# An attention and feed-forward block on one core: the steps written out over the images, another order around the taps, and one feature stream across images

## What is computed

```python
qkv = conv2d(layernorm_c(x), qkv_w)                    # 1x1, 768 channels
agg = conv2d(qkv, agg_dw_w, groups=768, padding=2)     # 5x5 depthwise
agg = conv2d(agg, agg_pw_w, groups=96)                 # 1x1, grouped
q, k, v = relu, relu, id of the thirds of concat(qkv, agg), heads of 8; v gets a column of ones
out = q @ (k^T v);  out = out[:-1] / (out[-1] + eps)
x = x + batchnorm(conv2d(out, proj_w))
t = layernorm_t(tokens of x)
w = expert weights from softmax(mean(t) @ router^T), top 2
x = x + sum_e w_e (gelu(t @ W1_e + b1_e) @ W2_e + b2_e)    # 6 experts, 341 wide
```

## Time and profile before

| | |
|---|---|
| device time, median of 3 runs | 1735.21 us |
| lowest, highest | 1733.52, 1737.08 us |
| span of the profiled execution | 1727.4 us (its own device time is not listed; the median is 7.8 us over the span) |
| mean granted clock of TensorE | 0.895 |
| PE busy | 1398.5 us, 81% |
| DVE busy | 1291.6 us, 75% |
| POOL busy | 1180.7 us, 68% |
| ACT busy | 931.2 us, 54% |
| chain that ended last | PE 44%, DVE 19%, POOL 18%, issue 13% |

### The profile page before, as it was taken

How to read it: one execution, slowest core, us unless ns; L and a number is a source line. 1 busy time by engine, 2 the same in 40 slices (tenths; PEclk the granted TensorE clock), 3 DMA queues, 4 the chain that set the end, 5 groups by cost and what they waited for, 6 DMA issues and landing times.

```text
span 1727.4 us, 20194 instructions
## 1 busy us (share of the span) xinstructions
PE 1398.5 (81%) x6652; PEld 793.5 (46%) x6652; DVE 1291.6 (75%) x1305; ACT 931.2 (54%) x1622; POOL 1180.7 (68%) x1017
## 2 busy tenths in 40 slices
PE   5414657569998899979997899879997899798998
PEld 2113455345463545445553645445544446454443
DVE  3999999999948997789958995799868896600100
ACT  3443434365646665655565564655666564544554
POOL 3573356347966797768875697768874677467776
PEclk7657777788999999989998899989998899898999
DMA  5100000000000100010001000010001000100000
GB/s 172 73 0 25 1 0 25 0 1 1 25 13 1 37 25 13 1 37 25 13 1 39 1 25 13 1 37 1 13 1 37 1 1 13 37 1 1 25 1 25
DMA packets 14270, 32.92 MB, mean 19 GB/s; under 512 B 2384, under 2 KB 5328, under 8 KB 13904
## 3 DMA queue, kind: packets, MB, share of 16 engines
q1 hardware_dynamic: 14160, 31.56, 5.2%
HBM read 23.17 MB, written 8.39 MB: 18 GB/s over the span
## 4 chain that ended last, share of the span: by engine, by line
PE 44%; DVE 19%; POOL 18%; issue 13%; ACT 4%; DMA 1%; POOLq 0%; ACTq 0%; SPq 0%; DVEq 0%
PE wbk L618 17%; DVE dacc L1139 17%; PE acc L631 13%; POOL dwo L933 6%; PE wbk L567 3%; POOL nrm L888 3%; PE wbk L593 3%; POOL gl L968 2%; POOL hb L965 2%; PE wbk L557 2%; PE wbk L582 1%; PE wbk L535 1%; POOL nrm L863 1%; POOL rb L861 1%; ACT dwo L683 1%
## 5 line engine op out<-in xcount | busy, mean ns | idle before, releaser
L1139 DVE SCALAR_TENSOR_TENSOR dacc<-qkvs,dww,dacc 128x930 f32<-128x930 f32 (+4 forms) x954 | 1052.9, 1187 | 0.5 <-issue 0.5
L968 POOL TENSOR_TENSOR gl<-hb,gh 128x512 f16<-128x512 f32 x256 | 302.1, 1180 | 21.4
L933 POOL TENSOR_TENSOR dwo<-dwo,tapb 128x992 f32<-128x992 f32 (+1 forms) x104 | 239.2, 2300 | 83.5 <-ACT tapb L688 74.7
L816 ACT ACTIVATE hb<-wbk,b1s 128x512 f32<-128x512 f32 x256 | 176.0, 687 | 210.1 <-PE wbk L618 209.9
L965 POOL TENSOR_SCALAR hb<-hb,ewg 128x512 f32<-128x512 f32 x256 | 184.8, 722 | 148.0 <-ACT gh L706 147.7
L631 PE MATMUL acc<-gh,w2h 128*128 128x512 f16 x512 | 199.0, 389 | 55.4 <-POOL gl L968 55.0
L631 PE MATMUL acc<-gh,w2l 128*128 128x512 f16 x512 | 198.5, 388 | 0.0
L631 PE MATMUL acc<-gl,w2h 128*128 128x512 f16 x512 | 198.5, 388 | 0.0
L706 ACT ACTIVATE gh<-hb,ewg 128x512 f16<-128x512 f32 x256 | 182.3, 713 | 0.0
L618 PE MATMUL wbk<-th,w1h 128*128 128x512 f16 x512 | 159.7, 395 | 4.9 <-ACT sum_b L802 2.4
L1027 DVE RECIPROCAL den<-den 128x128 f32<-128x128 f32 x32 | 30.4, 950 | 176.0 <-ACT den L791 176.0
(11 more groups left out here) (148 smaller groups left out, 2243.0 us busy)
## 6 DMA issues: line engine op xcount, KB each, us to landing
xa<-x SPq DMA_DIRECT2D x8, 1024.0 KB, 5.0
yr<-x SPq DMA_DIRECT2D x8, 1024.0 KB, 5.0
out<-yr SPq DMA_DIRECT2D x16, 512.0 KB, 2.8
dwo<-w SPq DMA_DIRECT2D x1, 2048.0 KB, 10.9
yr<-w SPq DMA_DIRECT2D x2, 1024.0 KB, 16.0
dwo<-w_qkv SPq DMA_DIRECT2D x1, 768.0 KB, 4.4
wp<-w_proj SPq DMA_DIRECT2D x1, 512.0 KB, 12.3
pw<-w_pw SPq DMA_DIRECT2D x16, 24.0 KB
```

The costliest lines, as they stand in the source:

```text
L816: last = nc.scalar.activation(hb[:, f % GB, :], b[:], ACT.Gelu, bias=b1s[:, f % FT:f % FT + 1], scale=1.0 / (X_SCALE * W_SCALE))
L933: ins = nc.gpsimd.tensor_tensor(d3[:, oy, ox], d3[:, oy, ox], t3[:, iy, ix], ALU.add)
L968: nc.gpsimd.tensor_tensor(gl[:, f % GB, :], hb[:, f % GB, :], gh[:, f % GB, :], ALU.subtract).then_inc(g_low, 1)
L1139: ins = nc.vector.scalar_tensor_tensor(out=dst[:, oy, ox], in0=i3[:, iy, ix], scalar=dww[:, m, tap:tap + 1], in1=a3[:, oy, ox], op0=ALU.mu ...
```

## The change

All steps are written out, as one list `ORDER` for all eight images, with constant semaphore values. Five things differ in it.

1. The taps take the pairs in the order 1, 2, 0: keys, values, queries. `agg` and the second `kv` of keys and values come while the query pair is still filtered. After the last tap only the query pair's `agg` and the attention product h 1 are left before the projection.
2. An iteration j works on the taps of image j, the second half of image j-1, the norm of image j+1, and features of images j-2 and j-1. The features are one stream: the first 14 of an image stand in the iteration in which the next image is filtered, from its logits on (10 for image 6), the others in the next one. Fewer stand in the first part: from `agg` of the query pair to `logits` there are 15.
3. The small tasks stand at n = 14 and 20 (reciprocals of h 1), 60 (`max`), 66 (`route`), all for the image before, and 92 and 97 (reciprocals of h 0).
4. The router's token mean comes with the activation that makes the high part (`accum_out`), not from a pass of its own (`usum`, L731).
5. `sum_b`, `nrm` and `acc` are guarded by the user just before in the list.

```diff
-def tap_order(first, pair):
-
-    skip = BASE_TAPS[:base_taps(first, 2 * pair)] + [CENTER, LAST_TAP]
+PAIRS = (1, 2, 0)
...
+    for j in range(-1, B + 2):
+        d, c, a = 0 <= j < B, 1 <= j <= B, 0 <= j + 1 < B
+        old, new = j - 2, j - 1
+        n = 3 if j == 0 else 1
+        if c:
+            agg(new, 0)
+            fill(1, old)
+            for t in range(TT):
+                based([("att", new, 1, t)])
+                if t % 2:
+                    fill(1, old)
+            give(("scale", new, 1))
+        if d:
+            qkv(j, 0, n)
+        if c:
+            fill(1, old)
+            based([("back", new, 1, ch, g) for ch in range(NCH) for g in range(2)])
+            fill(1, old)
+            based([("proj", new, ch, m) for ch in range(NCH) for m in range(CT)])
+            give(("squares", new, 1))
+            give(("sums", new, 1))
+        if d:
+            give(("relu_q", j))
+            for t in range(TT):
+                based([("tok", j, t)], n)
+                if t % 2:
+                    fill(1, old)
+        if c:
+            based([("stats", new, 1, 0)])
+            give(("rnorm", new, 1))
+            fill(2, old)
+            based([("rbc", new, 1, ch) for ch in range(NCH)])
+            give(("apply", new, 1))
+            fill(2, old)
+            give(("high", new, 1))
+            give(("low", new, 1))
+        if d:
+            based([("kv", j, 0, g) for g in range(2)], n)
+            give(("mask", j, 0))
+        if c:
+            based([("logits", new)])
+        fill(NCH * FT, old)
         if a:
...
+            give(("squares", j + 1, 0))
+            give(("sums", j + 1, 0))
...
+        if c:
+            give(("exp", new))
+        fill(2, new)
...
-            DIVIDE = {44: (2, 1, 0), 47: (2, 1, 1), 104: (1, 0, 0), 107: (1, 0, 1)}
-
-            CARRIED = {8: "max", 16: "route"}
-            OWN = {128: "max", 136: "route"}
...
+            OF_LAST = {14: ("rden", 1, 0), 20: ("rden", 1, 1), 60: ("max",), 66: ("route",)}
+            OF_THIS = {92: ("rden", 0, 0), 97: ("rden", 0, 1)}
```

More of the change, by code:

```diff
@@ L77, in schedule, with tap_ops, give @@
-def schedule(a, d, c, f):
+def tap_ops(s):
+    return [(pair, tap, m) for pair in PAIRS for tap in tap_order(s, pair) for m in (2 * pair, 2 * pair + 1)]
+def schedule():
     o = []
-    features = list(range(NCH * FT)) if f else []
-    todo = list(features)
+    waiting = []
+    stream = [(s, f) for s in range(B) for f in range(NCH * FT)]
+    todo = list(stream)
+    given = set()
+    def give(it):
+        o.append(it)
+        given.add(it)
     def second(k):
-        n = features[k]
-        o.append(("second", n))
+        s, n = stream[k]
+        give(("second", s, n))
@@ L89, in second, with fill @@
         if n % FT == FT - 1:
-            o.append(("final", n // FT))
-    def ffn(k):
+            give(("final", s, n // FT))
+    def fill(k, s):
         for _ in range(k):
[L94 to L208, removed]
-        if a:
[L210 to L214, removed]
+            if not todo or todo[0][0] > s:
+                return
+            i = len(stream) - len(todo)
+            n = todo.pop(0)
+            assert ("low", n[0], 1) in given
@@ L215, in schedule @@
+    k = len(stream)
+    assert not todo
+    give(("gsplit",) + stream[-1])
+    for i in range(k - LAG, k):
+        second(i)
     return o
+ORDER = schedule()
 BANKED = ("qkv", "agg", "kv", "stats", "rbc", "att", "back", "proj", "tok", "logits", "ffn")
-def fills(order):
-    return {it: n for n, it in enumerate([it for it in order if it[0] in BANKED])}
-def past(s, k):
-    return not isinstance(s, int) or s >= k
+FILL = {it: n for n, it in enumerate([it for it in ORDER if it[0] in BANKED])}
@@ new lines, with taps_before, taps_done, norm_before @@
+BASE_NO = {it[1:]: n + 1 for n, it in enumerate([it for it in ORDER if it[0] == "base"])}
+def taps_before(s, pair):
+    done = sum(len(tap_ops(i)) for i in range(s))
+    return done + sum(2 * len(tap_order(s, p)) for p in PAIRS[:PAIRS.index(pair)])
+def taps_done(s, pair):
+    return taps_before(s, pair) + 2 * len(tap_order(s, pair))
+def norm_before():
+    runs = [(it[1], it[2]) for it in ORDER if it[0] == "squares"]
+    return dict(zip(runs[1:], runs))
+def sum_b_before():
+    users, prev, table = {}, {}, {}
+    for it in ORDER:
+        if it[0] == "proj":
+            prev, slots = dict(users), [it[3]]
+        elif it[0] == "final":
+            prev, slots = dict(users), range(CT)
+        else:
+            continue
+        for m in slots:
+            table[it[:2] + (it[2], m, it[0])] = prev.get(m)
+            users[m] = (it[0], it[1], it[2])
+    return table
```

917 lines of the change are left out of this document (445 added, 472 removed).

## The result

| | before | after |
|---|---|---|
| device time, median of 4 runs each | 1734.37 us | 1769.95 us |
| lowest, highest | 1732.77, 1737.08 | 1768.52, 1771.08 |
| ratio, 95% interval | | 1.0203 (1.0189 to 1.0218) |
| span of the profiled execution | 1727.4 us | 1768.7 us |
| mean granted clock of TensorE | 0.895 | 0.883 |

What follows compares the result with a forecast made beforehand. Neither VectorE nor TensorE is simply full; in-order queues make them wait for one another. Images 2 to 7 +28.5, image 1 +17.3, tail -34.3 sum to +11.5: 1747 us, range 1695 to 1800 (forecast alone 1732 to 1770).

Steps and rivals of the forecast that it cites:

- Image 1: Image 1's window: now holds image 0's maximum and route, logits at 80 (58 to 94), 172.5 us instead of 155.2, +17.3.
- The period: Last tap to last tap in images 2 to 7: 97.2 + 11.9 + 7.0 + 78.3 = 194.4 us, against 189.65 before.
- the sum of 97.2 us: Last tap to router logits: the earlier measured 88.8 us, with terms taken off and added, gives 97.2 us.
- The six ready-made taps: ACT copies and POOL sums between query copies and transposes lengthen the way to the logits by 1.5 us, from 0 to 6.
- The clock: TensorE pauses some 5 to 8 us before the chain and runs slow after it: 3 us added, from 0 to 7.
- The measured chain of 88.8 us: Image 7 before the change, last tap to logits with 15 features: 88.8 us, the base for the new chain.
- Route and centre taps: On VectorE, priced from the earlier trace: route 7.0 us, two centre taps 3.1 us in the last pair.
- The tail: Last tap to the end: logits after 70.5 us, 43 features left instead of 48; 196.8 us against 231.1, -34.3.
- Rival 1: TensorE's slow clock doesn't add up: period 188.4 us, image 1 some 7 us shorter, 1704 us; chance 0.20.
- Rival 2: Features hide all latencies, TensorE's work alone sets the chain: 1639 us; chance 0.12 including what lies toward rival 1.
- Rival 3: The projection, 14 us at full speed, falls into the slow clock as back copies starve TensorE; slower; chance 0.18.
- Rival 4: VectorE is not held at the maximum, logits come before tap 60; excluded by 80.5 > 67.7 except in image 1.

Runs made afterwards that it cites:

- e1_max72: The changed kernel with the router's maximum at tap instruction 72 instead of 60 and the route at 78 instead of 66: 1707.26 us, ratio 0.9861.
- e5_base_later: The changed kernel with pair 0's ready-made taps given from the projection on instead of among the four transposes back: 1741.53 us, ratio 1.0050.
- e14_warm: The changed kernel with 22 more TensorE products, their result overwritten, ahead of each image's wait for its last taps: 1757.23 us, ratio 1.0135.
- e4_no_stream: The changed kernel with each image's 32 features all in one iteration, as before the change: 1789.97 us, ratio 1.0337.
- e11_72_squares_base: The changed kernel with maximum and route at 72 and 78, squares behind four token transposes, and ready-made taps from the projection on: 1668.40 us, ratio 0.9629.
- e12_exp_first: The changed kernel with the router's exponentials ahead of the next image's squares in ACT's queue: 1765.57 us, ratio 1.0188.

## Why the prediction was right in its mechanism and wrong in its size

- **Where the change costs: right.** The maximum stands ahead of its own logits. Forecast 25 to 33 us at the maximum, 3 to 6 at the route, `den` below 2: measured 29.99, 4.14 and none. Image 1's wait at the maximum was 11.36 us (some 12 forecast). `e1_max72` shows the cause by taking 63 us off with two numbers. Three signs lay just outside in part: last taps up to 199.7 us apart (192 to 198), the last image's wait at the route 2.26 us, and a tail of 204.6 us (190 to 203).
- **The period, 194.4 forecast, 198.15 measured: the step that failed is the sum of 97.2 us from the last tap to the logits.** The period is off by 3.75 us in each of six images, and that is three quarters of the 29.8 us. In the mean of the six the parts are: maximum 100.3 us behind the last tap instead of 97.2; maximum to route 11.1 instead of 11.9; route 7.5 instead of 7.0; the rest 79.2 instead of 78.3. So the first sum holds most of it. Two of its terms were sized too small and one was left out:
  - "The six ready-made taps between the query copies and the transposes: +1.5". `e5_base_later` moves these taps, and the logits come 5.1 us earlier; 2.0 of that is the clock of the projection, so 3.1 or more are the waits themselves (the query products took 0.7 us longer there). I had 0 to 6 and chose near the lower end because ACT and POOL are idle a third of the time; but in these microseconds their queues are not idle, and the last POOL sum (809.00) and `tapb` stand directly ahead of the last copy in the chain.
  - "The clock ... I add 3". In the rows of the chain the query products have +1.67, the projection +1.72 and the slow feature +2.72, so 6.1. `e14_warm` fills one pause: where that makes the first two fast, the logits come 3.3 us earlier.
  - The measured chain of 88.8 us was cut at 1585.10, where the logit product starts; in the kernel before the maximum started at 1586.09. The 1.0 us for product and copy is in no term.

  Counted once, these are 3.1 + 6.1 + 1.0 = 10.2 us or more against 4.5. The sum was short by only 3.1, so the rest of the chain was, by the difference, some 2.6 us too large; which hop, no run shows.
- **Route and centre taps** were priced at lengths of the earlier trace rows. The same instructions took longer in the new order: the route 3.4 us in image 1, where POOL is idle beside it, 7.8 to 8.6 in images 2 to 6 and 5.5 in image 7; centre taps 2224 ns in the mean against 1610. Only those of the last pair count (4.74 us for two instead of 3.10), as VectorE waits behind the others anyway. Route and rest together are 2.9 us over my terms in the image shown and 1.4 in the mean.
- **Image 1: 169.4 against 172.5.** Its maximum started 80.6 us behind the last tap, 80 forecast; as the bounds were 58 to 94, that close a hit is luck. What is off is the route, 3.4 us and not 7.0.
- **The tail: 204.6 against 196.8, a gain of 26.5 instead of 34.3.** The logit product started 76.4 us behind the last tap (1640.50), not 70.5. Slow query products (5.60 us) are 1.8 of that. The sums of the norm were slow too (6.97), but they were so in the chain that the 70.5 came from, and add nothing. The larger part is POOL's: from the end of its `rb` (1627.22) to its last `nrm` (1639.18) 12.0 us pass, with the splits of two features and a sum between them, and 7.5 before (1572.33 to 1579.79); the logit product waits 3.4 us for the high parts (`th`) made from it. The stream's own share, measured by `e4_no_stream`, is 25 us at the tail and 5 the other way before it.
- **Rival 1 (1704), the clock that doesn't add up:** refuted. Mean grants stay at 0.92 to 0.93 in the steady windows. The 6.1 us of the image shown, in six images, would be 37 us, 2.1% of the span (an estimate from one image's rows); one filled pause per image brings 12.7 us, 0.7%, back. The rule I set beside it (the Trainium skill, TensorE: Matmul & The Clock Gate, Part 1) keeps the ramp under 1% of the span. The one pause I tested agrees with that size; the estimate for the whole chain does not, and there the measured rows decide. Since my whole error was 1.3%, terms of this size have to be counted when two orders of one kernel are compared. The load of the function table again shows no drain: it ends at 883.52 and the exponential starts at 883.53.
- **Rival 2 (1639), everything hidden:** refuted for this order, though `e11_72_squares_base` went 101 us towards it.
- **Rival 3, the projection in the slow clock:** half true. In four of the six images it starts slow, behind a wait of TensorE of 2.2 us, but its 15.71 us are only 1.7 over the fast length. **Rival 4**, no hold at the maximum, is excluded by waits of 30.0 to 30.8 us in each of images 2 to 7.

## What to carry to other kernels

A small task that waits, placed at a count in an in-order engine's stream, has to be priced against the chain that feeds it: 12 taps of 138 decided between 1.4% faster and 2% slower than before. A chain measured once must be cut at the same event as the one it stands for. Too late costs as well, behind the task: the wait that went came back at the next one, or at another engine's queue. When single waits lie on one loop, fix them together: their gains here nearly added up.

## What the runs showed of the hardware

Some of VectorE's instructions stretch beside POOL's. The route among image 4's taps in the changed kernel on VectorE, then POOL at the same time:

```profile
884.89 2.07 DVE L995 TENSOR_SCALAR rt<-rt 128x2 f32<-128x2 f32 x1
887.00 2.94 DVE L998 TENSOR_SCALAR wsel<-iota,rt 128x11 f32<-128x11 f32 x2
```
```profile
884.59 2.35 POOL L810 TENSOR_TENSOR rb<-xa 128x1024 f32<-128x1024 f32 x1
886.90 2.35 POOL L812 TENSOR_TENSOR nrm<-nrm 128x1024 f32<-128x1024 f32 x1
889.22 0.69 POOL L912 TENSOR_SCALAR hb<-hb,ewg 128x512 f32<-128x512 f32 x1
```

An operation on two columns takes 2.07 us and ends at 886.96, 0.02 us behind the end of POOL's instruction that started before it. A reciprocal at 884.69, beside the same POOL instruction, took its usual 0.16 us. In image 1, where POOL was idle, the same two groups took:

```profile
294.36 0.23 DVE L995 TENSOR_SCALAR rt<-rt 128x2 f32<-128x2 f32 x1
294.63 0.49 DVE L998 TENSOR_SCALAR wsel<-iota,rt 128x11 f32<-128x11 f32 x2
```

The centre taps, which read two tiles of the on-chip memory (`qkvs` and `dwo`), took 2224 ns against 1610 before; the other taps, which read one there and `dacc` in the accumulation memory, stayed at their length (1191 ns in the mean against 1187). The Trainium skill (SBUF — State Buffer, SBUF: two separate sides, and Who interferes with whom) states that VectorE and GpSimd share a port pair by an exclusive lock held for a whole instruction, and that VectorE takes it for an operation in a two-port mode, which `tensor_scalar` can enter, and for one with two inputs there when GpSimd's operation reads there too. The rows agree with it: the stretched rows above are TENSOR_SCALAR, and the centre taps have two inputs there. No run isolated it, so it stays the best reading and is not shown; that `e14_warm` and `e12_exp_first` lost part of their gain in just these instructions fits too.
